# Seventeen instead of eighteen of 28 columns fetched by TensorE, and another order of the candidates in PSUM, in a graph network's narrow passes

## What is computed

```
def _L0_gnn_ref(x, edge_weight, src, dst):
    m = jnp.tanh(x[src] * edge_weight[:, None])
    return jax.ops.segment_sum(m, dst, num_segments=x.shape[0])

def _L2_gnn_ref(inputs, timestamp, W, b, src, dst):
    msg = inputs[src] * timestamp
    h = jax.ops.segment_max(msg, dst, num_segments=inputs.shape[0])
    return h @ W.T + b

def _L3_gnn_ref(x, edge_index, eps1, ...):
    ...
        agg = jax.ops.segment_sum(x[src], dst, num_segments=n_nodes)
    ...

x = _layernorm(x + _L0_gnn_ref(x, edge_weight, src, dst), axis=-1)
x = _layernorm(x + _L1_gnn_ref(x, edge_attr_16, ...), axis=-1)
x = _layernorm(x + _L2_gnn_ref(x, edge_weight1, ...), axis=-1)
x = _layernorm(x + _L3_gnn_ref(x, edge_index, ...), axis=-1)
```

## Time and profile before

| what | us |
|---|---|
| median of 3 runs | 8105.31 |
| lowest and highest | 8102.64, 8106.66 |
| profiled execution, span | 8106.3 |
| TensorE busy | 7107.4 (88%) |
| VectorE busy | 6896.2 (85%) |
| GpSimd busy | 5221.6 (64%) |
| ScalarE busy | 2239.6 (28%) |

### The profile page before, as it was taken

How to read it: one execution, slowest core, us unless ns; L and a number is a source line. 1 busy time by engine, 2 the same in 40 slices (tenths; PEclk the granted TensorE clock), 3 DMA queues, 4 the chain that set the end, 5 groups by cost and what they waited for, 6 DMA issues and landing times.

```text
span 8106.3 us, 209725 instructions
## 1 busy us (share of the span) xinstructions
PE 7107.4 (88%) x77871; PEld 6661.2 (82%) x77871; DVE 6896.2 (85%) x12224; ACT 2239.6 (28%) x7389; POOL 5221.6 (64%) x4570
## 2 busy tenths in 40 slices
PE   5999985999999999999995399998599996899994
PEld 5999984777777787777774399998599996899994
DVE  7999985999999999999997688888588885788884
ACT  0000003666666666666664100000000000000000
POOL 3555557888888888888886555555555555455554
PEclk9999997999999999999997699999799998899997
DMA  2223222555555555555554211111111111111110
GB/s 84 85 87 88 84 56 81 159 158 159 159 160 160 160 160 160 159 158 158 159 160 134 65 49 46 48 49 40 36 49 45 49 49 28 43 49 49 49 45 22
DMA packets 738222, 757.28 MB, mean 93 GB/s; under 512 B 153760, under 2 KB 698336, under 8 KB 738112
## 3 DMA queue, kind: packets, MB, share of 16 engines
q1 hardware_dynamic: 592640, 667.34, 24.9%
q0 software_dynamic: 140528, 86.77, 7.1%
q10 hardware_dynamic: 5008, 2.59, 0.1%
HBM read 239.80 MB, written 519.73 MB: 94 GB/s over the span
## 4 chain that ended last, share of the span: by engine, by line
PE 42%; DVE 29%; issue 23%; POOL 4%; DMA 1%; DVEq 1%; ACT 0%; ACTq 0%; another core or an unknown queue 0%; POOLq 0%; SPq 0%
PE ps L823 42%; DVE amax_room L1232 7%; DVE spare L1237 4%; DVE flat L1259 3%; DVE flat L954 2%; POOL got L456 2%; DVE msg L1137 2%; DVE stt L954 2%; DVE spare L1241 1%; DVE run L1158 1%; DVE wide_buf L954 1%; DVE raw L954 1%; POOL wide_buf L456 1%; DVE junk L1164 1%; DVE wide_buf L1116 1%
## 5 line engine op out<-in xcount | busy, mean ns | idle before, releaser
L456 POOL DMA_INDIRECT msg<-feat,cidx x1680 | 1681.5, 1001 | 1594.4 <-PE ps L823 1109.8
L823 PE MATMUL ps<-parts,wide_buf 128*128 128x160 bf16 x30240 | 2128.9, 233 | 289.0 <-DVE wide_buf L1116 276.4
L823 PEld LDWEIGHTS ps<-parts,wide_buf 128*128 128x128 bf16 x30240 | 2102.5, 98 | 304.8 <-issue 288.2
L456 POOL DMA_INDIRECT hsrc<-feat,aidx x1568 | 1921.5, 1225 | 461.1 <-issue 445.5
L823 PE MATMUL ps<-parts,flat 128*128 128x160 bf16 x30240 | 2118.5, 233 | 29.7 <-DVE flat L1116 16.7
L823 PEld LDWEIGHTS ps<-parts,flat 128*128 128x128 bf16 x30240 | 2093.3, 98 | 43.1 <-DVE flat L1116 21.4
L870 PEld LDWEIGHTS ps<-wsb,zT 102*128 102x128 f32 x9408 | 1462.9, 190 | 217.8 <-ACT zT L690 196.3
L870 PE MATMUL ps<-wsb,zT 102*128 102x192 f32 (+1 forms) x9408 | 1539.8, 313 | 99.0 <-ACT zT L690 98.5
L954 DVE TENSOR_TENSOR raw<-ps,amask 128x960 f32<-128x960 f32 x448 | 738.4, 1657 | 468.1 <-PE ps L823 286.5
L1137 DVE TENSOR_REDUCE msg<-raw 128x288 f32<-128x2880 f32 x224 | 1129.9, 5044 | 7.7
L657 ACT ACTIVATE cidx<-sidx 128x10 int32 (+1 forms) x224 | 46.8, 211 | 3684.6 <-DMA msg<-feat,cidx 3065.6
(11 more groups left out here) (220 smaller groups left out, 5229.9 us busy)
## 6 DMA issues: line engine op xcount, KB each, us to landing
state_tab<-flat SPq DMA_DIRECT2D x784, 512.0 KB
raw<-quot_tab SPq DMA_DIRECT2D x224, 576.0 KB
run_tab<-run SPq DMA_DIRECT2D x224, 224.0 KB
top_tab<-spare SPq DMA_DIRECT2D x392, 128.0 KB
msg<-feat,cidx POOLq DMA_INDIRECT x1680
hsrc<-feat,aidx POOLq DMA_INDIRECT x1568
efs<-in_ef SPq DMA_DIRECT2D x392, 34.0 KB
msg<-in_x,cidx POOLq DMA_INDIRECT x560
```

The source lines that it names most:

```text
L456: return pool.indirect_dma_start(dest, None, table, rows_at(idx))
L823: last = nc.tensor.matmul(block.rearrange("p (q c) -> p q c", c=D), hot[s][:, m, t * P:(t + 1) * P], parts[:, m * Q:(m + 1) * Q, part, :], ...
```

## The change

1. R goes from 18 to 17, so A goes from 10 to 11. A set has 255 matmuls instead of 270 and eleven gathers instead of ten; the one-hots are made for 17 columns (2176 elements instead of 2304).
2. The candidate index becomes the innermost one. `parts` is stored as (block, part, feature, candidate), a matmul reads 160 adjacent elements, PSUM and `picked` hold the ten candidates of a feature side by side, and the sum reads adjacent numbers.
3. Eleven shared columns no longer fill four banks evenly. The second multiply becomes two, first the two columns of the last bank (`s_rest`), then the nine of the other three (`s_share`); TensorE waits for both before column 6, VectorE before its sum.
4. `split` makes the new order in `junk` first: a memset, two copies, then the five operations as before, now on 800 elements.
5. `wide_buf` and `flat` shrink to 7168 floats each; GpSimd's memset of the padding of `parts` goes.

```diff
-R = 18
+R = 17
+BANKS = OWN // CB
+LAST = (R - OWN) % CB
+WIDE = 4 * DC * DD
...
-        parts = sb("parts", [P, MB * Q, 3, D], BF)
+        parts = sb("parts", [P, MB, 3, D, Q], BF)
...
-        picked = raw[:, R * P:R * P + R * QW].rearrange("p (r q c) -> p r q c", q=Q, c=D)
+        picked = raw[:, R * P:R * P + R * QW].rearrange("p (r c q) -> p r c q", q=Q, c=D)
...
                         if t == OWN and not (first and s == 0):
+                            pe.wait_ge(s_rest, n * NG + 2 * j + s)
                             pe.wait_ge(s_share, n * NG + 2 * j + s)
...
-                                    block.rearrange("p (q c) -> p q c", c=D),
-                                    hot[s][:, m, t * P:(t + 1) * P], parts[:, m * Q:(m + 1) * Q, part, :],
+                                    block.rearrange("p (c q) -> p c q", q=Q),
+                                    hot[s][:, m, t * P:(t + 1) * P], parts[:, m, part],
...
-                link(v.tensor_copy(parts[:, 0:NB, 0, :], features[:]))
-                link(tt(nt[:], features[:], parts[:, 0:NB, 0, :], ALU.subtract))
-                link(v.tensor_copy(parts[:, 0:NB, 1, :], nt[:]))
-                link(tt(nt[:], nt[:], parts[:, 0:NB, 1, :], ALU.subtract))
-                v.tensor_copy(parts[:, 0:NB, 2, :], nt[:]).then_inc(s_parts, 1)
+                left = junk[:, 0:MB * QW].rearrange("p (m c q) -> p m c q", c=D, q=Q)
+                whole = NB // Q
+                link(v.memset(left[:, whole], 0.0))
+                link(v.tensor_copy(left[:, 0:whole], features[:, 0:whole * Q].rearrange("p (m q) c -> p m c q", q=Q)))
+                link(v.tensor_copy(left[:, whole, :, 0:NB - whole * Q], features[:, whole * Q:NB].rearrange("p q c -> p c q")))
+                link(v.tensor_copy(parts[:, :, 0], left))
+                link(tt(left, left, parts[:, :, 0], ALU.subtract))
+                link(v.tensor_copy(parts[:, :, 1], left))
+                link(tt(left, left, parts[:, :, 1], ALU.subtract))
+                v.tensor_copy(parts[:, :, 2], left).then_inc(s_parts, 1)
...
-                    def picked_rows(lo, hi):
-                        return picked[:, lo:hi].rearrange("p (b t) q c -> p b (t q) c", t=CB)
-
                     def mask_rows(lo, hi):
-                        return amask[:, lo:hi].rearrange("p (b t) q -> p b (t q)", t=CB).unsqueeze(3).to_broadcast([P, (hi - lo) // CB, CB * Q, D])
+                        return amask[:, lo:hi, :].unsqueeze(2).to_broadcast([P, hi - lo, D, Q])
 
                     dve.wait_ge(q["pick"][s], (done + j) * A + OWN * A // R + 1)
-                    tt(picked_rows(0, OWN), mine_banks[s].rearrange("p b (r c) -> p b r c", c=D), mask_rows(0, OWN),
-                       ALU.mult).then_inc(q["read"][s], 1)
+                    tt(picked[:, 0:OWN], mine_banks[s], mask_rows(0, OWN), ALU.mult).then_inc(q["read"][s], 1)
                     dve.wait_ge(q["pick"][s], (done + j + 1) * A)
-                    tt(picked_rows(OWN, R), shared.rearrange("p b (r c) -> p b r c", c=D), mask_rows(OWN, R),
-                       ALU.mult).then_inc(s_share, 1)
+                    tt(picked[:, R - LAST:R], shared[:, (R - OWN) // CB, 0:LAST * QW], mask_rows(R - LAST, R), ALU.mult).then_inc(s_rest, 1)
+                    tt(picked[:, OWN:R - LAST], shared[:, 0:(R - OWN) // CB], mask_rows(OWN, R - LAST), ALU.mult).then_inc(s_share, 1)
+                    dve.wait_ge(s_rest, n * NG + 2 * j + s + 1)
                     dve.wait_ge(s_share, n * NG + 2 * j + s + 1)
                     dve.wait_ge(q["read"][s], done + j + 1)
-                    hold(v.tensor_reduce(msg[:, s, A:U, :], picked.rearrange("p r q c -> p r c q"), AX.X, ALU.add))
+                    hold(v.tensor_reduce(msg[:, s, A:U, :], picked, AX.X, ALU.add))
```

15 lines of the change are left out of this document (8 added, 7 removed).

## The result

| | median, us | lowest, highest |
|---|---|---|
| before | 8105.16 | 8102.64, 8106.66 |
| after | 8191.58 | 8187.88, 8194.27 |

The change makes the kernel **1.0% slower**: ratio 1.0104, 95% interval 1.0092 to 1.0117. The forecast was 7827 us, 3.4% faster. It is wrong in sign and far outside its range. The profiled execution of the changed kernel spans 8190.3 us and can stand for the median. One execution of a later experiment, e13, took 17,028 us; it is left out of that ratio, and its cause is open.

A forecast was written before the change was run, and what follows sets the result against it. TensorE was taken to bound passes 1 to 3 and VectorE's own chain pass 0. Terms -174.3 - 104.7 - 8.2 + 8.0 = -279 took 8106 to 7827 us (-3.4%), range 7791 to 7910.

The forecast's parts named there:

- GpSimd, one gather more: GpSimd's eleventh gather: no cost on the path, covered by VectorE's second and third multiply and reduce; margin 3.2 us.
- TensorE 17.63 + 0.14: Set period in passes 1 to 3: 255 matmuls in 17.63 us plus 0.14 of hiccups, 17.77 us.
- rare hiccups: TensorE in passes 1 to 3: 0.1 to 0.2 us between 18.67 and 18.81 a set, 0.14 carried into the forecast.
- One column less, 15 matmuls of 69.15 ns: TensorE saves 1.04 us a set; over passes 1 to 3 that makes -174.3 us.
- rival C: Matmuls gain from the adjacent operand, 66.7 ns each; about 7700 us in all; chance 0.03.
- The reduce: VectorE's sum over candidates, now along adjacent elements: 2.99 us instead of 5.04, -2.06 us a set.
- rival A: The reduce stays slow at 4.76 us and pass 0 stays VectorE's at 19.2; about 7909 us; chance 0.11.
- The multiplies and one-hots: VectorE: split multiply 0.49 and 1.66 us, together 2.15 against 2.16; five smaller one-hots save 0.2 us.
- Pass 0 passes from VectorE to TensorE: Pass 0: VectorE's chain falls to 17.5 us, TensorE binds, period 19.72 to 17.85 us, -104.7 us.
- Rival B: Pass 0 misses TensorE's pace, three engines being within 2 us: 18.4 us a set, 7858 us; chance 0.07.
- Ends of the passes: After each pass's last matmul: faster reduce, -8.2 us in all; longer split, +2.0 us four times, +8.0 us.
- Rival D: GpSimd's queue becomes the bound, gather issues at 1.82 us: 23.3 us a set, 9180 us; chance 0.02.

The follow-up runs named there:

- e13: Changed kernel, gathers waiting for no signal, GpSimd writing a scratch tile of 485 elements behind each; ratio 1.0029.
- e1: Kernel before with one column moved from TensorE to a gather (17 fetched, 11 gathered), candidates in their old order; 8110.49 us, ratio 1.0022.
- e3: Changed kernel with ten signals a set instead of eleven, the first two gathers going together; 8171.09 us, ratio 1.0095.
- e5: Changed kernel with its eleven gathers started in pairs, six signals a set; 8239.87 us, ratio 1.0139.
- e9: Changed kernel with the first gather of a set also waiting for the end of TensorE's set before; 8159.53 us, ratio 1.0061.
- e8: Changed kernel with every second gather left out, six a set, five columns of messages staying zero; 7802.13 us, ratio 0.9601.
- e2: Changed kernel with R back at 18 (ten gathers), so the new candidate order alone; 8069.28 us, ratio 0.9970.
- e15: Changed kernel (17 columns), gathers waiting for no signal, scratch write of 430 elements behind each, starts 1.588 us apart; ratio 0.9921.
- e16: e2's kernel (18 columns), gathers waiting for no signal, scratch write of 430 elements behind each, starts 1.591 us apart; ratio 0.9922.
- e7: e2's kernel with its ten gathers in two runs of five, the first behind the end of the set before; 9506.3 us, ratio 1.1699.
- e6: e2's kernel with its ten gathers in pairs behind five signals, the first behind the end of the set before; ratio 0.9990.
- e4: Changed kernel with two signals a set and gathers that wait for none of them, eleven back to back; 10382.04 us, ratio 1.2827.

## Why the prediction was wrong, point by point

**The step that failed** is "GpSimd, one gather more": "Cost on the path: nothing, the cover being these three." I priced the gather on its own engine and in VectorE's wait for it. There it is indeed covered: in the changed kernel VectorE has no wait for a gather in any pass. But gathers that lie close also take time from TensorE, and no wait in the profile names them. With eleven gathers the signals come 1.60 us apart, where ten had 18.67 / 10 = 1.87 us, and the first gather of a set follows right behind the last of the set before. Late gathers now close up into chains (the median distance is 1.37 us), and behind the third of a chain TensorE stops. That turned "TensorE 17.63 + 0.14" into 17.63 + 1.4 to 1.6. In numbers: 56 x (19.08 + 19.21 + 19.21 - 3 x 17.77) = +235 us, pass 0 56 x (20.52 - 17.85) = +150, together +385 against a miss of 365. The rest of 20 us is nearly the attention stage between passes 0 and 1, which came out 19 us shorter (3405 us from the last reduce of pass 0 to the first of pass 1, before 3424). Nothing in it changed. Over all runs it takes 3404 to 3448 us, and the five with eleven signal-paced gathers (after, e1, e3, e5, e9) are the five shortest, so it may be more than scatter; its cause is open.

The clue was in the trace before. I called its 0.1 to 0.2 us a set "rare hiccups" and carried them over as a constant. In passes 1 to 3, eight tenths of them without the clock's share stand behind the third and later gathers of chains, some 230 ns behind each, against 1 behind first ones. A residue should have been asked what it follows, before it was added. Nor did my list of signs hold one for this: none of the four that would have shown the forecast wrong (a slow reduce, waits for the one-hots in pass 0, waits for gathers, matmuls at 67 ns) came, only the periods were off.

**Point by point, the rest.**
- *One column less, 15 matmuls of 69.15 ns*: right. The period of e8 is 17.65 us. The matmuls still begin 69.2 ns apart with the new operand order, as taken; rival C is out.
- *The reduce*: right, 2.99 us forecast, 2.986 measured; rival A is out. e2 has 3.15 for 2880 elements, against 5.04 in the old order; e1, in the old order with 2720, has the 4.75 that the prediction had as its upper bound.
- *The multiplies and one-hots*: right, 0.491 and 1.647 us, and 3.57 us for five one-hots.
- *Pass 0 passes from VectorE to TensorE*: right in the direction, but TensorE's pace was 20.5 us and not 17.85. e8 has 17.90 with thin gathers, so the term of -104.7 us was sized well for a kernel without stops. Rival B (18.4 us) named pass 0 and three engines near each other; it missed passes 1 to 3, where most of the loss lies, and the cause.
- *Ends of the passes*: the reduce as forecast; the split costs 1.4 us more, not 2.0. Its copy of 640 elements reads 64 bytes apart and takes 0.72 us, not 1.28 (the row below). So the 1.75 ns an element of the reduces L1137 and L1384 do not hold for every read at such a distance.

```profile
5792.01 0.72 DVE L974 COPY junk<-xa 128x640 f32<-128x640 f32 x1
```

- *Rival D, slower by GpSimd*, with its chance of 0.02, had the right engine and sign, and the wrong mechanism and size (9180 us). GpSimd did not become the bound: it is busy 66%, a gather takes 986 ns in the mean in passes 1 to 3, and VectorE waits for TensorE and not for gathers. Slower than before should have had far more than 0.02, since the change loads an engine whose effect on the others the trace before showed only at one rate.

## What to carry to other kernels

Before adding an indirect DMA to a stream beside a busy TensorE, look at the distances between the starts of such DMAs and at TensorE's unexplained idle time behind close ones, not at the issuing engine's busy share. Here a run of gathers cost nothing while they started 1.59 us apart or more; closer ones were free only for the first few after a pause. A least distance (a small write behind each) held where signals did not, since a late gather lets the next ones close up. Even so the eleventh gather gained nothing over the tenth (e15 and e16). And time a change of two parts in its parts: the order of the elements gained 0.3% (0.8% with the gathers spaced), while moving one column to an eleventh gather lost 1.3%.

## What the runs showed of the hardware

- Gathers of GpSimd that follow one another closely make TensorE stand still in the midst of matmuls that wait for nothing. Two or three in a row at 1.25 us were free after a pause, from the fourth it was about 1 us each (e7: 0.00 behind the third, 1.0 and 1.3 behind the fourth and fifth). At an even 1.56 us the stops began at the eighth gather of a set and grew; at 1.59 there were none. This fits a backlog that is worked off at one gather in somewhat under 1.59 us. That is a reading; no trace here shows such a queue, and the stops are larger than the shortfall (at 1.44 us up to 1.0 us behind a gather).
- It is not a general halt. In the changed kernel 51 stops of over 0.2 us fall into VectorE's scans, which begin a median of 176 ns apart and never over 266. SyncE and GpSimd do show something. Of SyncE's DMA issues in passes 1 to 3 that overlap such a stop, 27 of 79 took over 0.5 us, of the others 14 of 566; of the rows below the second is a long one, which reaches just into the stop before 5093.04 (the timeline of SyncE after):

```profile
5090.89 0.35 SPq L333 DMA_DIRECT2D run_tab<-run  x1
5091.60 0.70 SPq L326 DMA_DIRECT2D raw<-quot_tab  x1
```

  GpSimd starts a gather that is not in a chain a median of 0.82 us behind the end of the matmul that signals it in the kernel before, and 2.34 us in the changed one. What the three share is open: nothing was run on it, nor with gathers of another size. The fetching of instructions, as far as the profile records it, is not the reason: its instruction queues move 58 packets in the whole execution after, against 714 stops of over 0.2 us, and none between 4662 and 5681 us, where pass 1 has its stops.
- The Trainium skill ("SBUF — State Buffer", "Who interferes with whom") says: "PE and ACT never wait on anyone", and that a DMA never contends with a compute engine. Read as a rule on SBUF ports it may stand, since the stops need not come from there. As a rule for a schedule the measurement goes against it, by 17% in e7 against e6.
- Stops cost twice. In e4, with TensorE busy 77% of the time, the granted clock is 0.80 to 0.85 in stretches of 100 us (1.2 GHz in part of them), where e8 has 1.00. Of the 11.2 us a set that its count gives in passes 1 to 3, 2.3 to 2.4 us are matmuls at 133 ns instead of 69, so about a fifth of the loss is the clock's. In e7 it is 1.7 to 2.3 us of 6.3 to 6.9.
